# A graph-attention and feed-forward kernel: own rows added on TensorE, the merge of block ends beside the last store, both stages in one program block

## The chip, the core and the metric

The kernel runs on one core of a Trainium2 chip. The metric is the device time of one execution in microseconds. A core has five engines with a queue of instructions each: TensorE (PE in the profile), VectorE (DVE), ScalarE (ACT), GpSimd (POOL) and SyncE (SP), which here only issues transfers. They synchronise by semaphores.

## What is computed

`x` holds 6250 nodes of 256 features, and 206,250 directed edges, sorted by destination, join them. Stage one is a graph attention with four heads of 64, stage two 30 passes of a small feed-forward scan.

```python
x = x + relu(gat(layernorm(x)) + bias)
#   h = layernorm(x) @ W; e = leaky_relu(a_src[src] + a_dst[dst])
#   alpha = softmax of e over the edges of one dst; out[dst] = sum of alpha * h[src]
def step(h):                       # 30 times, starting from layernorm(x)
    h = h + 0.01 * tanh(h)
    h = h * sigmoid(h)
    h = layernorm(h) * w + b
    return h @ W.T + bias
x = x + scan(step)
```

## The kernel before

Stage one, `attention`. Each of the 128 partitions owns 1612 consecutive edges. In 124 steps of 13 edges POOL gathers the rows `haug[src]` into `G`, and DVE and ACT turn them into running softmax sums within a node. SP stores every step's rows to `sums` in DRAM (L398), so that `sums` at a node's last edge holds its maximum, its weights' sum and its weighted rows. At the end ACT copies the last running row of each partition into `tail` (L514), and SP waits until the last stores have landed (L401). Then the block of `attention` ends, with a barrier of all engines (L882), and the block of `scan_ffn` begins.

The merge. A node whose edges begin in one partition and end in a later one needs the parts of the earlier partitions. POOL gathers the row concerned of each partition from `sums` into `last_row` (L1033). DVE, PE and ACT broadcast the tails' maxima over the partitions (`tdiag`, L1332), mask and reduce them (`tm`, `tmax`), take exponentials (`tw`), transpose them (L1336) and form the weighted sums of the tails (L1340). DVE scales and adds, and POOL scatters `fixed` back to `sums` (L1036). All the gathers that follow wait for this scatter.

The batches. The 49 nodes of each partition go in seven batches of seven tiles (a tile is 128 nodes, one in each partition). For a batch, POOL gathers seven rows `S` from `sums` (`ends`, L1043). DVE forms the softmax shares (`shares`, `norms`) with one exponential by ACT between them, and ends them with `partw`. The node's own row (its self loop) is loaded by SP into `own`, in three buffers (L1019). ACT scales it in place with 28 instructions (`own_part`, L1105), DVE scales the gathered sums into `Hs` (L1229) and adds `own` to `Hs` (L1234). Then `added` takes the relu and adds `X` (L1241), and takes statistics (L1244, L1248, L1251). POOL computes the root with four instructions (`roots`, L1050 to L1056), and ACT normalises (L1113). In POOL's queue `roots(b)` stands behind the gathers of batch b + 3; in ACT's queue `normalise(b)` stands behind `own_part(b + 2)`.

The loops. 25 chunks of two tiles (the last has one) run 30 times: tanh on ACT (L1143), an add on POOL (L1072), silu on ACT (L1128), transposes on PE (L1348), a copy on ACT (L1133), the product on PE (L1356), statistics on DVE, the root on POOL (L1081) and the affine step on DVE (L1285).

The core of the two lines that the batches turn on:

```python
v.tensor_tensor(hs, hs, tile_heads(own[:, b % OW, :, :], HR), ALU.add).then_inc(s_agg, 1)        # L1234
ch.add(v.scalar_tensor_tensor(out=xs, in0=hs, scalar=0.0, in1=xs, op0=ALU.max, op1=ALU.add))     # L1241
```

## Time and profile before

| | |
|---|---|
| median of 3 runs | 4212.8 us (4206.08 to 4213.14) |
| the profiled execution | 4199.51 us, its span 4197.7 us |
| PE busy in the span | 1679.0 us (40%) |
| DVE busy | 3153.5 us (75%) |
| ACT busy | 2543.4 us (61%) |
| POOL busy | 3170.6 us (76%) |
| mean granted clock of TensorE | 0.704 |

Times in the rows below are microseconds from the start of the span. The profiled execution took 1.8 us more than its span and 13.3 us less than the median of the runs. A view by stretch shows three parts: stage one up to about 2443.7 us, the merge and the batches up to about 2574 us, and the 30 passes of the loops behind them. The granted clock is a share of TensorE's 2.4 GHz: 0.5 is 1.2 GHz.

### The profile page before, as it was taken

The numbers are of one execution on the slowest core, as the hardware profiler recorded it, in microseconds if no ns is written. First come the engines' busy times: TensorE is split into PE (matmuls) and PEld (weight loads), VectorE is DVE, ScalarE is ACT, GpSimd is POOL, SyncE is SP. The second block draws the span as 40 slices with busy tenths as digits, with TensorE's granted clock in tenths as the row PEclk, the third lists the DMA queues.
The fourth block names the chain that finished last, engine by engine and source line by source line (L and its number), as shares of the span: only waits on it lengthen the run. The fifth ranks groups of instructions, "written<-read, shape, count | busy, mean of one in ns | idle before, by whom it ended". The sixth has DMA issues, their size and how long they took to land. (4 is left out here: it accounts for less than half of the span.)

```text
span 4197.7 us, 52564 instructions
## 1 busy us (share of the span) xinstructions
PE 1679.0 (40%) x9142; PEld 1465.3 (35%) x9142; DVE 3153.5 (75%) x7419; ACT 2543.4 (61%) x4454; POOL 3170.6 (76%) x3312
## 2 busy tenths in 40 slices
PE   3400000000000000000000004999999999999997
PEld 2300000000000000000000003888888888888886
DVE  6476667667666677766767758888888888888887
ACT  4354455545455555545555548777777777777775
POOL 7676666766666667766666748999999999999996
PEclk8655555555555555555555556999999999999998
DMA  6365556656555556555666641000000000000001
GB/s 192 118 206 180 175 194 208 200 184 197 184 192 196 188 196 217 189 176 191 199 198 199 216 140 31 1 0 0 0 0 0 0 0 0 0 0 0 0 0 61
DMA packets 126628, 485.80 MB, mean 116 GB/s; under 512 B 50089, under 2 KB 52170, under 8 KB 110532
## 3 DMA queue, kind: packets, MB, share of 16 engines
q0 software_dynamic: 83824, 230.16, 18.9%
q1 hardware_dynamic: 41188, 253.75, 16.6%
q10 hardware_dynamic: 1536, 1.18, 0.1%
q14 instruction: 74, 0.61, 0.0%
q8 instruction: 6, 0.10, 0.0%
HBM read 249.79 MB, written 235.99 MB: 116 GB/s over the span
## 5 line engine op out<-in xcount | busy, mean ns | idle before, releaser
L581 POOL DMA_INDIRECT G<-haug,idx x1612 | 1524.6, 946 | 717.0 <-issue 581.2
L1356 PE MATMUL ps_g<-WT,S 128*128 128x256 f32 x5880 | 1394.9, 380 | 0.0
L477 ACT ACTIVATE G<-RS 128x845 f32<-128x845 f32 x496 | 852.1, 1718 | 651.5 <-issue 479.9
L1356 PEld LDWEIGHTS ps_g<-WT,S 128*128 128x128 f32 x5880 | 1060.0, 190 | 113.5
L813 DVE TENSOR_TENSOR_SCAN RS<-keep,psum 128x845 f32<-128x845 f32 x496 | 941.4, 1901 | 0.4
L1072 POOL TENSOR_TENSOR S<-Hs,S 128x512 f32<-128x512 f32 (+1 forms) x750 | 938.3, 1251 | 3.3 <-ACT S L1143 3.2
L1332 PE MATMUL ps_x<-tdiag,ones 128*128 128x512 f32 x2 | 2.1, 1140 | 2274.9 <-DVE tdiag L1176 2274.9
L1285 DVE SCALAR_TENSOR_TENSOR Hs<-ps_g,r,b 128x256 f32 (+1 forms) x1470 | 683.5, 465 | 181.9 <-PE ps_g L1356 170.7
L1332 PEld LDWEIGHTS ps_x<-tdiag,ones 128*128 128x128 f32 x2 | 0.5, 309 | 2275.1 <-DVE tdiag L1176 2275.1
L1081 POOL TENSOR_TENSOR r<-cve,half_neg 128x2 f32<-128x2 f32 (+1 forms) x750 | 525.5, 701 | 147.0 <-DVE cve L1277 123.1
L1133 ACT ACTIVATE S<-ps_x 128x512 f32<-128x512 f32 (+1 forms) x750 | 441.0, 588 | 313.5 <-PE ps_x L1348 308.4
L1264 DVE BATCH_NORM_STATS2 cst<-S 128x6 f32<-128x256 f32 x1470 | 547.6, 412 | 10.0 <-issue 4.4
L795 DVE TENSOR_TENSOR psum<-G,psum 128x845 f32<-128x845 f32 x496 | 478.2, 1032 | 17.3 <-ACT psum L461 7.7
L1348 PE MATMUL ps_x<-ident,S 128*128 128x128 f32 x2940 | 445.2, 273 | 113.7 <-ACT S L1128 113.6
L1128 ACT ACTIVATE S<-S 128x512 f32<-128x512 f32 (+1 forms) x750 | 461.8, 616 | 33.5 <-POOL S L1072 26.1
L1143 ACT ACTIVATE S<-Hs 128x512 f32 (+2 forms) x750 | 461.0, 615 | 4.3
L804 DVE SCALAR_TENSOR_TENSOR psum<-carried,KEEP,psum 128x260 f32<-128x260 f32 x123 | 60.7, 494 | 526.6 <-remote 452.3
L1348 PEld LDWEIGHTS ps_x<-ident,S 128*128 128x128 f32 x2940 | 368.6, 141 | 190.9 <-ACT S L1128 115.1
L472 ACT ACTIVATE carried<-RS,decay 128x65 f32<-128x65 f32 x492 | 157.9, 392 | 224.4 <-remote 209.4
L1277 DVE TENSOR_SCALAR cve<-cmv 128x2 f32<-128x2 f32 (+1 forms) x750 | 250.2, 334 | 1.1
L1271 DVE BATCH_NORM_AGGREGATE cmv<-cst 128x2 f32<-128x6 f32 x1470 | 175.8, 160 | 0.4
L461 ACT ACTIVATE psum<-el 128x56 f32<-128x56 f32 x124 | 27.8, 224 | 221.8 <-issue 151.4
(153 smaller groups left out, 1110.4 us busy)
## 6 DMA issues: line engine op xcount, KB each, us to landing
sums<-G SPq DMA_DIRECT2D x124, 1716.0 KB
G<-haug,idx POOLq DMA_INDIRECT x1612
haug<-G SPq DMA_DIRECT2D x7, 924.0 KB
own<-haug SPq DMA_DIRECT2D x7, 924.0 KB, 4.7
X<-x SPq DMA_DIRECT2D x7, 784.0 KB
out<-X SPq DMA_DIRECT2D x7, 784.0 KB
adz<-G SPq DMA_DIRECT2D x4, 830.5 KB
G<-adz SPq DMA_DIRECT2D x1, 3224.0 KB, 11.5
```

The lines of the kernel that those rows point to most:

```text
L477: nc.scalar.activation(G[:, k % R, :, h * HR:(h + 1) * HR].rearrange("p t f -> p f t"), RS[:, h, :, :], ACT.Copy).then_inc(s_rows, 1)
L581: pool.indirect_dma_start(out=G[:, u, t, :], out_offset=None, in_=haug[:, :], in_offset=bass.IndirectOffsetOnAxis(ap=idx[:, u, t:t + 1], a ...
L795: ch.add(v.tensor_tensor(ps_m[:, h, :, :].rearrange("p f t -> p t f"), G[:, u, :, h * HR:(h + 1) * HR], w, ALU.mult))
L813: v.tensor_tensor_scan(RS[:, h, :, :].rearrange("p f t -> p (f t)"), keep[:, k % 2, :, :].rearrange("p f t -> p (f t)"), ps_m[:, h, :, :]. ...
L1072: g.tensor_tensor(h1[:, u, 0:w * C], chunk_rows(Hs, j0 + u, w), th[:, u, 0:w * C], ALU.add).then_inc(s_add, 1)
L1081: g.tensor_tensor(r100[:, u, 0:w], cve[:, u, 0:w], half_neg[:, 0:w], ALU.pow).then_inc(s_r, 1)
L1128: nc.scalar.activation(h2[:, u, 0:w * C], h1[:, u, 0:w * C], ACT.Silu, scale=1.0 / HS).then_inc(s_silu, 1)
L1143: nc.scalar.activation(th[:, u, 0:w * C], chunk_rows(Hs, j0 + u, w), ACT.Tanh, scale=1.0 / HS).then_inc(s_tanh, 1)
L1264: last = v.bn_stats(cst[:, u, a, :], h2[:, u, a * C:(a + 1) * C])
L1285: ins = v.scalar_tensor_tensor(out=Hs[:, bass.ds(j * CH + a, 1), :].rearrange("p a c -> p (a c)"), in0=ps_g[u][:, a * C:(a + 1) * C], scal ...
L1348: last = nc.tensor.transpose(ps_x[XB[u]][:, n * P:(n + 1) * P], h2[:, u, n * P:(n + 1) * P], ident[:, :])
L1356: last = nc.tensor.matmul(ps_g[u][:, a * C:(a + 1) * C], h2T[:, u, (a * 2 + k) * P:(a * 2 + k + 1) * P], WT[:, k, :], start=(k == 0), stop ...
```

## The change

Four edits. (1) The two blocks become one: `attention` and `scan_ffn` return their five queue programs, and one block runs one behind the other on each engine, without a barrier between. (2) The merge becomes the end of `attention`. Its scratch tiles lie in a part of `AD`. It takes the exponentials against the earlier partitions' own maximum `tmax`, so that they don't need `last_row`, and rescales both parts with `escale` afterwards. POOL itself waits for the stores. SP, POOL and DVE wait for `s_merged` at the start of stage two, so that the loads of `own`, which had been issued at the start of the second block, now come behind the merge. (3) DVE no longer adds `own` to `Hs`: TensorE multiplies the identity with the rows of `Hs` and of `own` into the same PSUM region (14 products a batch), and the relu reads this sum. The order of DVE's work becomes `gathered(b)` and then `added(b - 1)`. (4) The scale of the root moves into DVE's `ve`, and the sign of the mean into a new `nmean`, so that `roots` has two instructions in place of four. PSUM is laid out anew for the loops, and the first transposes and the first product wait until the batches' sums are read.

```diff
-        attention(nc, sem, res, dram, x, src, dst, gW, att_src, att_dst, gbias, ln_w, ln_b, fW, fb)
-        scan_ffn(nc, sem, res, dram, out)
+        *attend, s_merged = attention(nc, sem, res, dram, x, src, dst, gW, att_src, att_dst, gbias, ln_w, ln_b, fW, fb)
+        iterate = scan_ffn(nc, sem, res, dram, out, s_merged)
+        with nc.Block() as block:
+            @block.sync
+            def _(sp):
...
+                attend[0](sp)
+                iterate[0](sp)
...
-            for u in range(R):
-                sp.wait_ge(s_st[u], TURNS * 16)
...
+        def gpsimd_fix(pool):
+            for u in range(R):
+                pool.wait_ge(s_st[u], TURNS * 16)
+            pool.indirect_dma_start(out=last_row, out_offset=None, in_=sums[:, :],
+                                    in_offset=bass.IndirectOffsetOnAxis(ap=e1_idx[:, 0:1], axis=0)).then_inc(s_e1, 16)
+            pool.wait_ge(s_fixed, 1)
+            pool.indirect_dma_start(out=sums[:, :], out_offset=bass.IndirectOffsetOnAxis(ap=e1_idx[:, 0:1], axis=0),
+                                    in_=fixed, in_offset=None).then_inc(s_merged, 16)
...
+        def scalar_fix(act):
+            act.wait_ge(s_tlog, 1)
+            nc.scalar.activation(tw, tm, ACT.Exp).then_inc(s_tw, 1)
+            act.wait_ge(s_twT, 1)
+            nc.scalar.activation(twT.rearrange("p h q -> p (h q)"), ps_twT, ACT.Copy).then_inc(s_twc, 1)
+            act.wait_ge(s_ediff, 1)
+            nc.scalar.activation(escale, ediff, ACT.Exp).then_inc(s_escale, 1)
...
+            dve.wait_ge(s_tail, 1)
+            for h in range(H):
+                last = v.tensor_scalar(tdiag[:, h, :], ident[:, :], tail[:, SUMS + h:SUMS + h + 1], None, ALU.mult)
+            last.then_inc(s_tdiag, 1)
+            dve.wait_ge(s_trow, 1)
+            ch.add(v.tensor_tensor(tm, ps_trow.rearrange("p (h q) -> p h q", h=H),
+                                   maskneg[:, :].unsqueeze(1).to_broadcast([P, H, P]), ALU.add))
+            ch.wait()
+            v.tensor_reduce(tmax, tm, axis=AX.X, op=ALU.max).then_inc(s_tmax, 1)
+            dve.wait_ge(s_tmax, 1)
+            v.tensor_tensor(tm, tm, tmax.unsqueeze(2).to_broadcast([P, H, P]), ALU.subtract).then_inc(s_tlog, 1)
+            dve.wait_ge(s_e1, 16)
+            ch.add(v.tensor_tensor(emax, tmax, last_row[:, SUMS:ROW], ALU.max))
+            ch.wait()
+            v.tensor_tensor(ediff[:, 0, :], last_row[:, SUMS:ROW], emax, ALU.subtract)
+            v.tensor_tensor(ediff[:, 1, :], tmax, emax, ALU.subtract).then_inc(s_ediff, 1)
+            v.tensor_copy(fixed[:, SUMS:ROW], emax)
+            dve.wait_ge(s_escale, 1)
+            v.tensor_tensor(heads(fixed), heads(last_row), escale[:, 0, :].unsqueeze(2).to_broadcast([P, H, HR]), ALU.mult)
+            dve.wait_ge(s_tsum, 1)
+            ch.add(v.tensor_tensor(heads(earlier), heads(ps_tsum), escale[:, 1, :].unsqueeze(2).to_broadcast([P, H, HR]), ALU.mult))
+            ch.wait()
+            v.tensor_tensor(fixed[:, 0:SUMS], fixed[:, 0:SUMS], earlier[:, 0:SUMS], ALU.add).then_inc(s_fixed, 1)
...
+        psum = ctx.enter_context(nc.psum_tensor("ps", [P, 8 * 512], F32))
+        assert QT * C <= 4 * 512 and NQ % 2 and U == 5
+        ps_sum = [psum[:, n * 2048:n * 2048 + QT * C] for n in range(2)]
+        ps_g = [psum[:, n * 512:(n + 1) * 512] for n in (0, 1, 2, 3, 7)]
+        ps_x = [psum[:, n * 512:(n + 1) * 512] for n in (4, 5, 6)]
...
+            sp.wait_ge(s_merged, 16)
...
+            pool.wait_ge(s_merged, 16)
...
+            def roots(b):
+                t0, t1 = part_tiles(b)
+                pool.wait_ge(s_x1var, b + 1)
+                ch.add(g.tensor_tensor(rstd[:, t0:t1], ve[:, t0:t1], half_neg[:, t0:t1], ALU.pow))
...
+                g.tensor_tensor(nmr[:, t0:t1], rstd[:, t0:t1], nmean[:, t0:t1], ALU.mult).then_inc(s_x1root, 1)
...
+            dve.wait_ge(s_merged, 16)
...
+            def gathered(b):
+                hs = tile_heads(Hs[:, b * QT:(b + 1) * QT, :], HID)
+                dve.wait_ge(s_part, b + 1)
+                v.tensor_tensor(hs, tile_heads(S[:, b * QT:(b + 1) * QT, :], HR),
+                                part[:, b % 2, 0, :, :].unsqueeze(3).to_broadcast([P, QT, H, HID]),
+                                ALU.mult).then_inc(s_scaled, 1)
...
+            def added(b):
+                t0, t1 = part_tiles(b)
+                xs = X[:, t0:t1, :].rearrange("p t c -> p (t c)")
+                dve.wait_ge(s_agg, b + 1)
+                v.scalar_tensor_tensor(out=xs, in0=ps_sum[b % 2], scalar=0.0, in1=xs, op0=ALU.max, op1=ALU.add).then_inc(s_added, 1)
+                dve.wait_ge(s_added, b + 1)
...
+                v.tensor_scalar(nmean[:, t0:t1], mv[:, t0:t1, 0], -1.0, None, ALU.mult)
+                v.tensor_scalar(ve[:, t0:t1], mv[:, t0:t1, 1], EPS, 1.0 / (HS * HS), ALU.add, ALU.mult).then_inc(s_x1var, 1)
...
+            for b in range(NQ):
+                shares(b)
+                norms(b)
+                gathered(b)
+                if b:
+                    added(b - 1)
+            added(NQ - 1)
...
+            def add_own(b):
+                pe.wait_ge(s_scaled, b + 1)
+                pe.wait_ge(s_ownw, b + 1)
+                wait_count(pe, s_added, b - 1)
+                for j in range(QT):
+                    to = heads(ps_sum[b % 2][:, j * C:(j + 1) * C], HID)
+                    nc.tensor.matmul(to, ident[:, :], heads(Hs[:, b * QT + j, :], HID), start=True, stop=False)
+                    last = nc.tensor.matmul(to, ident[:, :], heads(own[:, b % OW, j, :], HR), start=False, stop=True)
+                last.then_inc(s_agg, 1)
+
+            for b in range(NQ):
+                add_own(b)
...
+            def transposes(q, u, w):
+                if isinstance(q, int) and q == 0:
+                    pe.wait_ge(s_added, NQ - 1)
...
+            def product(q, u, w):
+                if isinstance(q, int) and q == 0:
+                    pe.wait_ge(s_added, NQ)
```

Rows of a queue are written as line, operation, output<-inputs and size. In the changed kernel the merge's scratch is named `AD`, and PSUM `psum` or `ps`; its line numbers are its own.

DVE, from the second batch on (batch 1 in the code), before: `partw` closes `norms(1)`, and then come `added(0)`, `gathered(1)` and the start of `shares(2)`.

```order
L1219 TENSOR_TENSOR partw<-share,den 128x56
L1241 SCALAR_TENSOR_TENSOR X<-Hs,X 128x1792
L1244 BN_STATS bst<-X 128x6 x7
L1248 BN_AGGR mv<-bst 128x2 x7
L1251 TENSOR_SCALAR ve<-mv 128x7
L1229 TENSOR_TENSOR Hs<-S,partw 128x1792
L1234 TENSOR_TENSOR Hs<-Hs,own 128x1792
L1205 TENSOR_TENSOR nmax<-S,eself 128x28
```

The same place on DVE in the changed kernel:

```order
L1273 TENSOR_TENSOR partw<-share,den 128x56
L1282 TENSOR_TENSOR Hs<-S,partw 128x1792
L1290 SCALAR_TENSOR_TENSOR X<-ps,X 128x1792
L1293 BN_STATS bst<-X 128x6 x7
L1297 BN_AGGR mv<-bst 128x2 x7
L1300 TENSOR_SCALAR nmean<-mv 128x7
L1301 TENSOR_SCALAR ve<-mv 128x7
L1259 TENSOR_TENSOR nmax<-S,eself 128x28
```

The addition of `own` is gone from DVE, the scaling of `S` stands ahead of the relu of the batch before, and the relu reads PSUM.

POOL, from the end of stage one to the second group of roots, before:

```order
L882 UNCONDITIONAL_BRANCH
L1029 UNCONDITIONAL_BRANCH
L1033 DMA last_row<-sums,e_idx 128x264
L1036 DMA sums<-fixed,e_idx 206337x264
L1043 DMA S<-sums,end_idx 128x264 x28
L1050 TENSOR_TENSOR rstd<-ve,half_neg 128x7
L1052 ISA
L1052 TENSOR_SCALAR rstd<-rstd 128x7
L1054 TENSOR_TENSOR nmr<-rstd,mv 128x7
L1056 TENSOR_SCALAR nmr<-nmr 128x7
L1043 DMA S<-sums,end_idx 128x264 x7
L1050 TENSOR_TENSOR rstd<-ve,half_neg 128x7
```

The same place on POOL in the changed kernel:

```order
L935 DMA AD<-sums,e_idx 128x264
L938 DMA sums<-AD,e_idx 206337x264
L1130 DMA S<-sums,end_idx 128x264 x28
L1137 TENSOR_TENSOR rstd<-ve,half_neg 128x7
L1139 TENSOR_TENSOR nmr<-rstd,nmean 128x7
L1130 DMA S<-sums,end_idx 128x264 x7
L1137 TENSOR_TENSOR rstd<-ve,half_neg 128x7
```

The branches out of and into a block are gone, and each group of roots has two instructions; the order of gathers and roots is the same.

PE, between stage one and the loops, before:

```order
L879 MATMUL psum<-bdiag,ones 128x128 x2
L882 UNCONDITIONAL_BRANCH
L1329 UNCONDITIONAL_BRANCH
L1332 MATMUL ps_x<-tdiag,ones 128x512
L1336 MATMUL ps_x<-ident,tw 128x128 x4
L1340 MATMUL ps_x<-tail,twT 128x65 x4
L1348 MATMUL ps_x<-ident,S 128x128 x12
```

The same place on PE in the changed kernel, up to the second tile of the first batch:

```order
L925 MATMUL psum<-bdiag,ones 128x128 x2
L951 MATMUL psum<-AD,ones 128x512
L954 MATMUL psum<-ident,AD 128x128 x4
L958 MATMUL psum<-tail,AD 128x65 x4
L1389 MATMUL ps<-Hs,ident 128x256
L1390 MATMUL ps<-own,ident 128x256
L1389 MATMUL ps<-Hs,ident 128x256
L1390 MATMUL ps<-own,ident 128x256
```

The pair of L1389 and L1390 comes 49 times in all, ahead of the first transposes of the loops.

## Rows read from the trace of the kernel before

**Rows 1.** Busy time by stretch: PE, PEld, DVE, ACT, POOL; then PEclk, DMA share, GB/s

```profile
2455.00:2458.00 3.00, 0.00 (x0) 0.00 (x0) 1.00 (x4) 0.25 (x2) 0.00 (x0) 0.50 1.03 430
...
2596.00:4171.00 1575.00, 1575.00 (x8724) 1388.16 (x8725) 1385.18 (x5100) 1222.19 (x2222) 1426.39 (x1483) 1.00 0.00 0
```

**Rows 2.** Timeline of the merge: start, duration, engine, line, operation, idle time before

```profile
2443.30 0.42 ACT L514 ACTIVATE tail<-G 128x264 f32<-128x264 f32 x1
...
2449.37 0.87 DVE L1176 TENSOR_SCALAR tdiag<-ident,tail 128x128 f32<-128x128 f32 x4 [7.85 <-PEq L882]
...
2453.13 0.69 DVE L1183 TENSOR_REDUCE tmax<-tm 128x4 f32<-128x512 f32 x1
...
2457.03 0.68 DVE L1190 TENSOR_TENSOR tm<-tm,emax 128x512 f32<-128x512 f32 x1
...
2458.50 0.43 DVE L1193 TENSOR_TENSOR fixed<-last_row,escale 128x260 f32<-128x260 f32 x1 [0.79 <-ACT tw L1091]
...
2460.33 1.97 PE L1340 MATMUL ps_x<-tail,twT 128*128 128x65 f32 x8 [0.69 <-ACT twT L1093]
...
2465.83 0.96 POOL L1043 DMA_INDIRECT S<-sums,end_idx  x1 [1.72 <-DMA sums<-fixed,e_idx]
```

**Rows 3.** Chain of work: start, duration of the merge's two transfers

```profile
2449.97 6.62 DMA last_row<-sums,e_idx
...
2463.11 2.46 DMA sums<-fixed,e_idx
```

**Rows 4.** Waits of SP's queue around the merge: total, times, longest

```profile
SPq L401 <- DMA sums<-G: 5.1, 1, 5.1
```

**Rows 5.** Timeline of one batch in the middle, all engines

```profile
2526.82 3.55 ACT L1113 ACTIVATE Hs<-X,nmr,rstd 128x256 f32<-128x256 f32 x7 [3.04 <-POOL nmr L1056]
...
2531.49 2.02 DVE L1241 SCALAR_TENSOR_TENSOR X<-Hs,X 128x1792 f32<-128x1792 f32 x1
2531.67 6.79 ACT L1105 ACTIVATE own<-own,partw 128x64 f32<-128x64 f32 x28 [1.17 <-issue]
2532.11 2.22 POOL L1043 DMA_INDIRECT S<-sums,end_idx  x1 [0.30 <-issue]
2533.54 2.39 DVE L1244 BATCH_NORM_STATS2 bst<-X 128x6 f32<-128x256 f32 x7
...
2536.66 2.02 DVE L1229 TENSOR_TENSOR Hs<-S,partw 128x1792 f32<-128x1792 f32 x1
2536.85 3.21 POOL L1050 TENSOR_TENSOR rstd<-ve,half_neg 128x7 f32<-128x7 f32 x1
2538.71 2.02 DVE L1234 TENSOR_TENSOR Hs<-Hs,own 128x1792 f32<-128x1792 f32 x1
...
2541.51 3.55 ACT L1113 ACTIVATE Hs<-X,nmr,rstd 128x256 f32<-128x256 f32 x7 [3.04 <-POOL nmr L1056]
```

**Rows 6.** Timeline of the last batch, POOL, ACT and DVE

```profile
2556.12 1.51 POOL L1050 TENSOR_TENSOR rstd<-ve,half_neg 128x7 f32<-128x7 f32 x1
...
2561.04 6.79 ACT L1105 ACTIVATE own<-own,partw 128x64 f32<-128x64 f32 x28 [1.17 <-DVE partw L1219]
...
2570.13 2.02 DVE L1241 SCALAR_TENSOR_TENSOR X<-Hs,X 128x1792 f32<-128x1792 f32 x1
```

**Rows 7.** Timeline of a step of stage one, DVE and POOL

```profile
2224.91 3.85 DVE L795 TENSOR_TENSOR psum<-G,psum 128x845 f32<-128x845 f32 x4
2225.47 0.94 POOL L581 DMA_INDIRECT G<-haug,idx  x1 [0.30 <-issue]
```

**Rows 8.** Timeline of PE at the start of the loops

```profile
2577.10 1.11 PE L1348 MATMUL ps_x<-ident,S 128*128 128x128 f32 x4 [0.26 <-ACT S L1128]
2578.01 3.62 PE L1356 MATMUL ps_g<-WT,S 128*128 128x256 f32 x8
...
2588.50 1.89 PE L1356 MATMUL ps_g<-WT,S 128*128 128x256 f32 x8
```

**Rows 9.** Stretches of 1 us, PE alone: busy, granted clock, DMA share, GB/s

```profile
2581.00:2582.00 1.00, 1.00 (x7) 0.67 0.00 0
```

683 lines of the change are left out of this document (315 added, 368 removed).

## The prediction

> **What bounds the kernel now.** I read the busy time by stretch first. In the loops PE is busy for 1575.0 of 1575 us at the full clock, while DVE, ACT and POOL have room [rows 1]. The change leaves the loops' instructions as they are, so nothing is to be had there, and the question is when the loops start. The timeline shows what lies ahead of them. Stage one ends with the copy of `tail` at 2443.72, the first gather of stage two starts at 2465.83 [rows 2], and the first product of the loops at 2578.01 [rows 8]. I count batch times from that first gather, as +x: the product is at +112.2.
>
> In the middle of the batches one batch takes 2541.51 - 2526.82 = 14.69 us [rows 5]. POOL has no idle time in it: seven gathers of 1.25 us (0.95 and 0.30 between) make 8.75; one that runs into a DVE instruction is stretched to 2.22, 1.27 more; and the roots take 2541.51 - 2536.85 = 4.66, of which 3.21 is the power. Sum 14.68. So POOL sets the pace. ACT needs only 3.55 + 1.30 (from the end of the normalisation to the start of `own_part`, for shares and norms) + 6.79 = 11.64 us [rows 5].
>
> **The merge.** Now it is a chain in series: the store lands 5.1 us after SP began to wait for it [rows 4], which I put at 2448.8; then come the barrier, the gather of `last_row` (6.62 us) and, behind it, subtraction, exponential, transposes and products, and the scatter (2.46 us) [rows 2, 3].
> In the new order two chains run side by side from 2443.72.
> - Tails: `tdiag` to `tmax` took 2453.82 - 2449.37 = 4.45, and the subtraction to the last product 2462.30 - 2457.03 = 5.27 [rows 2]. With 0.05 for starts this chain is done at 2453.5.
> - `last_row`: the store at 2448.8, then the gather. Its 6.62 us were spent beside three loads of `own` that filled the DMA engines (share 1.03 [rows 1]); the scatter of the same rows without them took 2.46 [rows 3]. The loads now come later, so I take 3.0 and keep 2.46 and 6.62 as bounds: 2451.8. Four small DVE instructions, an exponential and a scaling of 0.43 [rows 2] are put at 1.3 us: 2453.1.
>
> The tails end last, at 2453.5. Two DVE instructions of 0.43, 0.27 to start, 2.46 for the scatter and 0.26 to the first gather give 2457.4. Against 2465.83 this is **8.4 us**. With 6.62 for the gather it would be 5.3 us.
> The loads of `own` now start with the gathers and not 16 us ahead. I cost this at nothing: the first `own` is wanted only at +12.4 (below), and the first loads shared the DMA with `last_row` and that landed in 6.62. If the first batch came 2 us late for it, the next batches would absorb it, since ACT idles between `own_part(0)` and the shares of batch 1, which wait for gathers.
>
> **The batches.**
> - DVE loses one addition of 2.02 a batch. What counts is who waited on DVE's account. The power of 1.51 us [rows 6] takes 3.21 when it meets L1229 and L1234, and a gather takes 2.22 when it meets L1241 [rows 5]: each time DVE reads two SBUF operands. L1234 is gone, and L1241 now has one operand in PSUM. In stage one DVE's L795, with one operand in PSUM, runs for 3.85 us over a gather that takes 0.94 [rows 7]. So I let only L1229 stretch a gather, by 1.3 a batch, and the power stays at 1.51, since DVE runs no such instruction right behind `ve` any more. The Trainium skill, "SBUF — State Buffer", section "Who interferes with whom", says that a VectorE instruction with at most one SBUF input leaves GpSimd alone, and the trace agrees. The same section infers that a `tensor_tensor` does not hold up the descriptors of a GpSimd transfer. By that the gathers would never be stretched, and the POOL cycle below would be 1.3 us shorter; the 2.22 us speak against it.
> - Roots: 4.66 becomes 1.51 + 0.08 + 0.21 and a start, 1.85 us. `nmean` adds 0.1 on DVE, beside POOL's gathers.
> - POOL's cycle: 8.75 + 1.3 + 1.85 = 11.9. ACT's: 11.64. I take 12.0.
> - PE: a batch has 14 products of 256 columns. Four of them (eight instructions) show 1.89 us at the full clock and 3.62 at half [rows 8], with an end that overlaps the next; in a row of 14 I take 0.44 and 0.88 each. At the start of the loops the clock rose at about 2581.6, 4.6 us after work without gaps began at 2577.10 [rows 8, 9]. If it does so in each addition, 4.6 us give 5.2 products and the other 8.8 take 3.9: **x = 8.5 us**. Bounds: 6.2 all at full, 12.3 all at half.
> - Is the addition on the path? It starts when `own_part(b)` ends. Then come x us for it, 2.05 for the relu, 3.4 for statistics and variance, 0.5 for the shares of batch b + 2, 1.3 to the start of their `own_part` and 6.8 for that: x + 14.1 for two batches. With x = 8.5 that is 11.3 a batch, under 12.0. It becomes the bound from x = 9.9.
>
> Times: 28 gathers with three stretched take 38.9; with `roots(0)`, normalisation(0) starts at +41, ends at +44.6, and `own_part(3)` starts at +45.9. Three cycles later `own_part(6)` starts at **+81.9**; before, it was 2561.04, +95.2 [rows 6].
>
> **The start of the loops.** `own_part(6)` ends at +88.7, the addition at +97.2, the relu at +99.3, and the first product may start at +99.4, 12.8 us earlier than +112.2. But DVE is not as far: before, its last relu ended at 2572.15, +106.3 [rows 6], now at +99.3, 7.0 us earlier, and statistics, variances and affine steps hang on it. POOL's addition for chunk 4 stands behind the root of chunk 0, which needs DVE. So the first products come earlier by 12.8, and then PE waits. By the fifth product I expect 9.1 us, between the bounds 7.0 and 12.8. From there PE is never idle in either kernel but for a wait of about 1 us.
>
> **Sum:** 8.4 + 9.1 = 17.5 us. The profiled execution's 4199.5 would become 4182.0, its span 4180.2. The median of the runs lies 13.3 higher: 4212.8 - 17.5 = **4195.3 us**, 0.42% less.
>
> **Rivals.** 0.2% is 8.4 us, about what a measurement of this kernel can tell from no change.
> - *The additions stay at half clock* (chance 0.12). Between two batches PE idles for some 3.5 us, and after long idle time it started the loops at half clock. x = 12.3: `own_part(6)` then ends at 19.2 + 3 * (x + 14.1) = +98.4, where 19.2 is the end of `own_part(0)` (seven gathers 8.75, landing 1.9, shares 1.8, and 6.8). That is 9.7 later than +88.7, and the last addition 3.8 longer: 17.5 - 13.5 = 4.0 us faster, 4208.8. Against it stands that the clock did rise within 4.6 us of steady work. The Trainium skill, "TensorE: Matmul & The Clock Gate", section "HAM oscillation — how this bites in real kernels", tells of kernels that fall back to the low clock in each gap and start each burst slowly; that is the forecast for each batch's first part, and this rival if the rise never comes.
> - *The additions stream more slowly than the loops' products* (0.07), and the kernel ends slower. Their operands and results are cut into four pieces of 64, `own` at a stride of 65, which no row shows. At twice the time, x = 14.6: +105.3, so 16.6 and 6.1 lost, 5.2 us slower than before, 4218.0. It decides from x = 13.3, and is slower by 0.2% from x = 15.4 (1.1 us a product). For it: nothing but the absence of a row. Against: L795 and L1229 show no price for such cuts, on another engine though.
> - *The merge gains little* (0.08): the gather of `last_row` is slow by itself. 5.3 + 9.1 = 14.4 us, 4198.4, inside the range.
> - *The loops run a little slower* (0.05): PSUM banks and the place of the code have moved. PE has 750 chunks (1575 us for 8724 / 12 = 727 of them, 2.17 each) with no slack at all [rows 1], so 23 ns a chunk eat the 17.5 us, and 35 ns make it slower by 0.2%. No row speaks for it.
> - The forecast: 0.68. Its own range is 4188 to 4203.
>
> **Numbers.** The range takes in the bounds of the merge (5.3 to 9), of the batches (POOL unstretched gives 2 us more) and of the loops' start (7.0 to 12.8), a few us between sets of runs, and reaches to the first rival: 4184 to 4209. Faster by over 0.2%: the forecast, the third rival and a part of the first, 0.80; within 0.2%: 0.14; slower: 0.06.
>
> **What would show it.** In the profile after: `tdiag` right behind `tail`, and the first gather of `S` 13.7 us behind `tail`; gathers over 2 us only beside the scaling of `S`, and powers of 1.5 us; 12 us from one normalisation to the next; additions of 8 to 9 us with the clock rising in each; a gap of PE after the second or third product. It is wrong if the additions take over 10 us, if DVE's relu from PSUM still holds up POOL, if the last store lands later than 2449, or if a chunk of the loops no longer takes what it did.

## The result, and the profile after

The changed kernel takes 4190.9 us, the median of 5 runs (4188.57 to 4197.38); the kernel before, run beside it, takes 4211.19 us (5 runs, 4206.08 to 4213.14). The ratio is 0.996, with a 95% interval of 0.9949 to 0.9972: faster by 0.3 to 0.5%. The forecast was 4195.3 us. One run of the kernel before, on the chip of e5_warm to e9_old_order below, took 6804.12 us where its other 19 took 3956 to 3961; it is a slow one and no ratio uses it.

Its profiled execution took 4197.38 us, its span 4195.2 us at a mean granted clock of 0.711. PE is busy for 1731.7 us, DVE for 3150.6, ACT for 2550.9, POOL for 3159.0.

The span is only 2.5 us shorter than before, and the reason lies ahead of the change. In this execution stage one ended 14.8 us later: the copy of `tail` ended at 2458.50, before at 2443.72 [rows 2]. Other kernels below, with the same stage one and on chips on which it ran as long, ended it anywhere from 2439.6 to 2457.6. So I compare executions from the end of `tail` on: 1753.98 us before, 4195.2 - 2458.50 = 1736.70 after, **17.28 us less; the sum of the prediction was 17.5**. Times "+x" count from the first gather of `S`, as in the prediction.

**The merge.** The timeline of the changed kernel:

```profile
2458.07 0.43 ACT L560 ACTIVATE tail<-G 128x264 f32<-128x264 f32 x1
...
2458.53 0.87 DVE L968 TENSOR_SCALAR AD<-ident,tail 128x128 f32<-128x128 f32 x4 [2.24 <-ACT tail L560]
...
2464.36 0.94 POOL L935 DMA_INDIRECT AD<-sums,e_idx  x1 [42.57 <-DMA sums<-G]
...
2466.23 1.97 PE L958 MATMUL psum<-tail,AD 128*128 128x65 f32 x8 [0.69 <-ACT AD L945]
...
2468.71 0.43 DVE L988 TENSOR_TENSOR AD<-AD 128x260 f32<-128x260 f32 x1
...
2472.14 0.97 POOL L1130 DMA_INDIRECT S<-sums,end_idx  x1 [1.73 <-DMA sums<-AD,e_idx]
```

The tails' work starts 0.03 us behind `tail`, while the last store is still on its way; before, it waited for the new block [rows 2]. The first gather comes 13.64 us behind `tail`, where it was 22.11. The chain of waits (start, duration, what) shows which of the two chains ends last:

```profile
2458.11 5.48 DMA sums<-G
...
2463.66 0.70 issue
2464.36 2.74 DMA AD<-sums,e_idx
...
2468.71 0.44 DVE AD L988
2469.15 0.27 issue
2469.41 2.47 DMA sums<-AD,e_idx
```

By this view it goes through the store and `last_row`. The products of the tails end at 2468.20, 0.06 us before the scaling of `last_row` does (2467.83 + 0.43 = 2468.26): the two chains end level, and which of them is last is too close to call, as the ends of products are modelled in the profile. The gather of `last_row` took 2.74 us, before 6.62 [rows 3]; the scatter 2.47, as before.

**The batches.** One batch in the middle:

```profile
2515.13 3.56 ACT L1189 ACTIVATE Hs<-X,nmr,rstd 128x256 f32<-128x256 f32 x7
...
2515.34 1.19 PE L1389 MATMUL ps<-Hs,ident 128*128 128x256 f32 x2 [7.21 <-issue]
...
2519.94 2.03 DVE L1282 TENSOR_TENSOR Hs<-S,partw 128x1792 f32<-128x1792 f32 x1
2520.00 6.82 ACT L1181 ACTIVATE own<-own,partw 128x64 f32<-128x64 f32 x28 [1.17 <-issue]
...
2520.82 1.97 POOL L1130 DMA_INDIRECT S<-sums,end_idx  x1 [0.31 <-issue]
...
2522.82 1.52 POOL L1137 TENSOR_TENSOR rstd<-ve,half_neg 128x7 f32<-128x7 f32 x1
...
2523.79 0.59 PE L1390 MATMUL ps<-own,ident 128*128 128x256 f32 x2
...
2524.42 2.02 DVE L1290 SCALAR_TENSOR_TENSOR X<-ps,X 128x1792 f32<-128x1792 f32 x1 [2.45 <-PE ps L1390]
2524.78 1.01 POOL L1130 DMA_INDIRECT S<-sums,end_idx  x1 [0.16 <-issue]
...
2526.71 3.57 ACT L1189 ACTIVATE Hs<-X,nmr,rstd 128x256 f32<-128x256 f32 x7
```

A batch takes 2526.71 - 2515.13 = 11.58 us, before 14.69 [rows 5]. The power takes 1.52 instead of 3.21. The gather that runs into the scaling of `S` (L1282, two operands in SBUF) is stretched to 1.97; the one that starts 0.36 us into the relu, which now reads PSUM (L1290), takes 1.01. This addition lasted from 2515.34 to 2524.38, 9.04 us; the others of this execution took 6.3 to 9.3. The granted clock, the sixth number behind the stretch and its length (PE, PEld, DVE, ACT and POOL busy stand between), shows why. The first three lines are of this addition, the next two of the one after it:

```profile
2517.00:2518.00 1.00, 1.00 (x3) 0.76 (x3) 0.90 (x9) 1.00 (x3) 0.94 (x1) 0.50 0.47 131
2520.00:2521.00 1.00, 1.00 (x4) 0.77 (x4) 1.00 (x1) 1.00 (x5) 0.69 (x2) 0.53 0.36 114
2521.00:2522.00 1.00, 1.00 (x6) 0.90 (x5) 0.97 (x1) 1.00 (x6) 1.00 (x1) 1.00 0.53 135
...
2525.00:2527.00 2.00, 0.08 (x1) 0.11 (x2) 1.97 (x3) 2.00 (x9) 1.70 (x2) 1.00 0.83 225
2528.00:2531.00 3.00, 3.00 (x9) 2.34 (x8) 2.52 (x17) 2.53 (x6) 2.21 (x3) 0.50 0.60 200
...
2600.00:4170.00 1570.00, 1570.00 (x8696) 1383.75 (x8694) 1391.82 (x5082) 1222.30 (x2212) 1423.32 (x1477) 1.00 0.00 0
```

The addition began at half clock (0.50 is 1.2 GHz) and had the full clock from about 2520.9, 5.6 us after its start. PE had idled for 7.2 us before it. The next one, at 2526.92 and behind 2.54 us of idle time, began at the full clock, fell to half some 0.8 us into its work and had the full clock again from about 2531.2, so that it took 7.96 us. The last line is the loops: PE has no idle time in them, as before [rows 1]. From the tenth product to the end of the span it is 1596.4 us, before 1596.9.

**The start of the loops.** PE in the changed kernel, and POOL's root of chunk 0:

```profile
2572.18 1.99 PE L1412 MATMUL ps<-WT,S 128*128 128x256 f32 x8 [0.23 <-DVE X L1290]
...
2574.45 1.89 PE L1412 MATMUL ps<-WT,S 128*128 128x256 f32 x8
...
2576.72 0.70 POOL L1164 TENSOR_TENSOR r<-cve,half_neg 128x2 f32<-128x2 f32 x1 [4.91 <-DVE cve L1327]
...
2579.38 1.12 PE L1402 MATMUL ps<-ident,S 128*128 128x128 f32 x4 [3.03 <-ACT S L1204]
2580.28 2.93 PE L1412 MATMUL ps<-WT,S 128*128 128x256 f32 x8
...
2586.36 1.89 PE L1412 MATMUL ps<-WT,S 128*128 128x256 f32 x8
```

The first product is at +100.0, 12.1 us earlier than before. Behind the second PE idles for 3.03 us, because POOL waited 4.91 us for DVE's variances of chunk 0, and the third product runs at half clock (2.93 us). The fifth is at +114.2, 8.5 us earlier.

### The profile page after: what moved, and what is told of

It reads as the page before. It is cut to its first block, busy times and chain, and to the rows that moved or that the text cites. A ratio compares the mean times of both kernels' runs of the same rounds, so it can differ in the third digit from the quotient of the medians.

```text
span 4195.2 us, 52930 instructions
## 1 busy us (share of the span) xinstructions
PE 1731.7 (41%) x9338; PEld 1508.3 (36%) x9338; DVE 3150.6 (75%) x7421; ACT 2550.9 (61%) x4454; POOL 3159.0 (75%) x3298
## 4 chain that ended last, share of the span: by engine, by line
PE 40%; DVE 16%; another core or an unknown queue 15%; issue 12%; POOL 8%; DMA 4%; SPq 2%; ACT 1%; DVEq 0%; ACTq 0%; POOLq 0%
PE ps L1412 30%; DVE RS L859 9%; PE ps L1402 8%; POOL G L627 8%; DVE psum L841 5%; DMA sums<-G 2%; SPq L399 1%; DMA G<-haug,idx 1%; PE psum L909 1%; PE ps L1389 1%; SPq L437 1%; PE ps L1390 1%; ACT G L523 0%; DVE bm L825 0%
## 5 line engine op out<-in xcount | busy, mean ns | idle before, releaser
L1412 PE MATMUL ps<-WT,S 128*128 128x256 f32 x5880 | 1394.2, 380 | 0.2 <-DVE X L1290 0.2
L1412 PEld LDWEIGHTS ps<-WT,S 128*128 128x128 f32 x5880 | 1059.7, 190 | 113.8 <-DVE X L1290 0.5
L1335 DVE SCALAR_TENSOR_TENSOR Hs<-ps,r,b 128x256 f32 (+1 forms) x1470 | 684.3, 466 | 172.0 <-PE ps L1412 161.5
L1164 POOL TENSOR_TENSOR r<-cve,half_neg 128x2 f32<-128x2 f32 (+1 forms) x750 | 526.4, 702 | 148.7 <-DVE cve L1327 124.4
L1209 ACT ACTIVATE S<-ps 128x512 f32<-128x512 f32 (+1 forms) x750 | 442.4, 590 | 307.6 <-PE ps L1402 301.1
L1402 PE MATMUL ps<-ident,S 128*128 128x128 f32 x2940 | 444.0, 273 | 5.2 <-ACT S L1204 4.7
L1402 PEld LDWEIGHTS ps<-ident,S 128*128 128x128 f32 x2940 | 368.5, 141 | 81.8 <-ACT S L1204 6.6
L1327 DVE TENSOR_SCALAR cve<-cmv 128x2 f32<-128x2 f32 (+1 forms) x750 | 262.9, 350 | 1.1
```

The lines of the kernel that those rows point to most:

```text
L1164: g.tensor_tensor(r100[:, u, 0:w], cve[:, u, 0:w], half_neg[:, 0:w], ALU.pow).then_inc(s_r, 1)
L1335: ins = v.scalar_tensor_tensor(out=Hs[:, bass.ds(j * CH + a, 1), :].rearrange("p a c -> p (a c)"), in0=ps_g[u][:, a * C:(a + 1) * C], scal ...
L1402: last = nc.tensor.transpose(ps_x[XB[u]][:, n * P:(n + 1) * P], h2[:, u, n * P:(n + 1) * P], ident[:, :])
L1412: last = nc.tensor.matmul(ps_g[u][:, a * C:(a + 1) * C], h2T[:, u, (a * 2 + k) * P:(a * 2 + k + 1) * P], WT[:, k, :], start=(k == 0), stop ...
```

## The experiments

They ran on three chips, on one of which stage one took some 250 us less; what is compared below stands on one chip, or is a distance within an execution. The columns: median of the runs, its ratio to the kernel before on the same chip with the 95% interval, then of the profiled execution the first gather behind `tail`, the end of the span behind `tail`, and the fifth and the tenth product of the loops behind the first gather. The kernel before had a median of 4208.41 us on the chip of e1 to e4, 3958.83 on that of e5, e6, e7 and e9, and 4211.63 on that of c1, e8 and e10.

| kernel | us | ratio | 1st gather | end | 5th | 10th |
|---|---|---|---|---|---|---|
| before | 4211.19 | 1 | 22.11 | 1753.98 | +122.7 | +135.0 |
| after | 4190.9 | 0.9960 [0.9949, 0.9972] | 13.64 | 1736.70 | +114.2 | +126.6 |
| e1_merge_only | 4201.44 | 0.9978 [0.9964, 0.9991] | 13.63 | 1744.39 | +123.1 | +135.3 |
| e2_undo_pe | 4196.51 | 0.9966 [0.9953, 0.9979] | 13.67 | 1742.81 | +120.6 | +132.9 |
| e3_undo_roots | 4195.23 | 0.9966 [0.9955, 0.9977] | 13.64 | 1738.97 | +116.7 | +129.2 |
| e4_loads_late | 4209.45 | 1.0002 [0.9992, 1.0011] | 19.26 | 1750.85 | +123.2 | +135.5 |
| e5_warm | 3940.88 | 0.9955 [0.9938, 0.9971] | 13.63 | 1735.52 | +112.0 | +124.4 |
| e6_reorder | 3944.01 | 0.9965 [0.9951, 0.9979] | 13.65 | 1739.52 | +110.8 | +129.4 |
| e7_double | 3959.69 | 1.0004 [0.9994, 1.0014] | 13.64 | 1754.49 | +132.0 | +144.4 |
| e9_old_order | 3968.54 | 1.0025 [1.0015, 1.0034] | 13.62 | 1762.75 | +140.3 | +152.7 |
| c1_after | 4195.1 | 0.9962 [0.9948, 0.9975] | 13.64 | 1738.28 | +117.1 | +127.9 |
| e8_warm_reorder | 4192.99 | 0.9959 [0.9946, 0.9973] | 13.64 | 1734.29 | +110.4 | +124.6 |
| e10_spread | 4189.26 | 0.9943 [0.9929, 0.9957] | 13.64 | 1731.47 | +110.8 | +121.6 |

Two executions of the same changed kernel (after and c1_after) differ by 1.6 us in the distance from `tail` to the end, so differences under about 2 us in that column say little by themselves.

**c1_after: the changed kernel once more**, without an edit, beside the last two.

> The changed kernel again. Theory: the stretch from the tail copy to the end of the span is 1736 to 1737.5 us as in its first profile (1736.70), and the end of stage one may lie anywhere within some 15 us, as it did for kernels with the same stage one. Rival (the change delays stage one, as the first profiles suggested): the tail copy ends about 15 us later than in the kernels with the old stage two.

It took 4195.1 us beside 4211.63, 16.5 us less. The additions took 6.3 to 9.2 us again, a batch 11.55. The distance from `tail` to the end, 1738.28 us, is 0.8 over the 1736 to 1737.5 that I expected, and its fifth product comes 2.9 us later than in after. 1.1 of them were there at the first product, since the last addition took 9.22 us for 7.76; behind it two products ran almost wholly at half clock (3.21 and 3.22 us) where after had one. The rival, that the change delays stage one, finds no support: `tail` ended at 2454.62 here, at 2454.05 in e4_loads_late with the old stage two, and at 2439.59 in e2_undo_pe, which has the new merge.

**e1_merge_only: the one block and the merge alone.** The additions are back on DVE, the old order and the old roots too.

```diff
             for b in range(NQ):
                 shares(b)
                 norms(b)
-                gathered(b)
                 if b:
                     added(b - 1)
+                gathered(b)
...
-            for b in range(NQ):
-                add_own(b)
```

> The changed kernel with DVE adding own and with four root instructions, so that only the merge and the single block are left of the change. My theory (two terms, 8.4 for the merge and 8.5 for the batches and the start of the loops): from the end of the tail copy to the first gather of S 13.6 us as in the changed kernel (22.1 before), from there to the fifth product 122.7 us as before (114.2 in the changed kernel); time 8 to 9 us under the kernel before. Rival (the single block also helps or hurts stage one or the loops): the two intervals are as said and the time is off by more than 5 us.

The first gather stands at 13.63 us, as in the whole change, and the batches are those of before: 14.70 us each, fifth product at +123.1. From `tail` to the end it is 9.6 us less than before, 8.5 of them ahead of the first gather. The rest of the gain, 7.7 us against after and 6.1 against c1_after, belongs to the other edits. The loads of `own` come behind the merge here too, and so the runs show what that costs: `own_part(0)` starts at +13.5, before at +12.3, and `own_part(6)` at +95.6, before at +95.2. With the additions on DVE 0.4 of the 1.2 us are left.

**e2_undo_pe: the additions back on DVE and the old order, with the new roots**

> The changed kernel with DVE adding own to Hs again, in the old order; merge and two-instruction roots stay. Theory (DVE's instructions with two SBUF operands hold POOL up, and POOL sets the pace): the power takes 2.6 to 3.2 us again, gathers over 2 us appear beside the relu, one batch takes 13.6 to 14 us against 11.7, and the fifth product comes 119 to 122 us after the first gather against 114.2. Rival (the roots' shorter chain was what gained): batches of about 12.5 us, fifth product at 116.

The edit is that of e1_merge_only, but for the roots, which stay at two instructions. A batch took 14.13 us, a little more than the 13.6 to 14 that I expected; the fifth product, at +120.6, is where I expected it. POOL and DVE in the middle of one:

```profile
2518.70 2.34 POOL L1130 DMA_INDIRECT S<-sums,end_idx  x1 [0.30 <-issue]
...
2523.43 2.02 DVE L1282 TENSOR_TENSOR Hs<-S,partw 128x1792 f32<-128x1792 f32 x1
2523.56 3.27 POOL L1137 TENSOR_TENSOR rstd<-ve,half_neg 128x7 f32<-128x7 f32 x1
2525.49 2.03 DVE L1287 TENSOR_TENSOR Hs<-Hs,own 128x1792 f32<-128x1792 f32 x1
```

The power meets the two DVE instructions with two SBUF operands each, and takes 3.27 us. So two POOL instructions fewer gave only 14.70 - 14.13 = 0.57 us a batch; the power of 1.5 us comes with the new place of the addition and the new order together. e9_old_order below parts the two.

**e3_undo_roots: the old four instructions of the root, the rest as changed**

```diff
-                g.tensor_tensor(nmr[:, t0:t1], rstd[:, t0:t1], nmean[:, t0:t1], ALU.mult).then_inc(s_x1root, 1)
+                ch.add(g.tensor_scalar(rstd[:, t0:t1], rstd[:, t0:t1], HS, None, ALU.mult))
+                ch.wait()
+                ch.add(g.tensor_tensor(nmr[:, t0:t1], rstd[:, t0:t1], mv[:, t0:t1, 0], ALU.mult))
+                ch.wait()
+                g.tensor_scalar(nmr[:, t0:t1], nmr[:, t0:t1], -1.0, None, ALU.mult).then_inc(s_x1root, 1)
...
```

On DVE `nmean` and the scale in `ve` go too.

> The changed kernel with four root instructions again. Theory: roots take 0.65 us longer on POOL, whose cycle of 11.7 is level with ACT's, so a batch takes 12.3 to 12.5 us and the fifth product comes 2 to 3 us later (116 to 117.5 us after the first gather). Rival (ACT alone sets the pace and POOL has room): batches stay at 11.7, fifth product within 1 us of 114.2.

A batch took 11.55 us at first and 12.7 later, 1.1 more than after; the power stays at 1.53. From `tail` to the end it is 2.3 us more than after, 0.7 more than c1_after. The start of `own_part(6)` shows it more clearly, since it lies ahead of the clock's ups and downs at the start of the loops: +84.6 here, +83.2 in after, +82.9 in c1_after, so that the new roots are worth 1.4 to 1.7 us there. The batch of 11.55 and then 12.7 us also tells the two limits apart. From one power to the next POOL takes 12.8 us, without idle time. As long as POOL was ahead, ACT set the pace; once the lead was used up, POOL did.

**e4_loads_late: the kernel before, with the loads of `own` behind the merge**

```diff
             def _(sp):
+                sp.wait_ge(s_merged, 16)
                 for b in range(NQ):
```

> The kernel before with one wait more: SP issues the loads of own behind the merge. Theory (the gather of last_row was slow only because it shared the DMA with them): it lands in 2.7 us in place of 6.6, the first gather of S comes 3.9 us earlier after the tail copy (18.2 us), and the time is 3 to 4 us less, so that nearly half of the merge's 8.4 us is had with one line. Rival (the wait hurts the first batch): first gather as said, but the fifth product later than 123.7 us after it, and no gain in time.

The timeline of its merge, POOL and DVE:

```profile
2460.28 0.95 POOL L1034 DMA_INDIRECT last_row<-sums,e_idx  x1 [43.47 <-POOLq L882]
...
2463.44 0.69 DVE L1184 TENSOR_REDUCE tmax<-tm 128x4 f32<-128x512 f32 x1
2464.16 0.16 DVE L1187 TENSOR_TENSOR emax<-tmax,last_row 128x4 f32<-128x4 f32 x1
```

The view of the tile gives 2.8 us from the issue to the landing of `last_row`, where it was 6.62 [rows 3]: the loads beside it were what made it slow. But the first gather comes only 22.11 - 19.26 = 2.85 us earlier: with the row there at about 2463.1, `emax` waits for `tmax`. The wait was hidden behind one that was nearly as long. From `tail` to the end it is 3.1 us less than before, 0.07%, which the interval of the ratio allows; the runs alone can't tell this kernel from before. The other 5.6 us of the merge's 8.5 come from the single block and from the tails' work beside the store, which no run took apart.

**e5_warm: TensorE kept busy between two additions**, with products of no use into free PSUM

```diff
+            def fill(b, count):
+                pe.wait_ge(s_added, b)
+                spare = psum[:, (1 - b % 2) * 2048 + QT * C:(2 - b % 2) * 2048]
+                for _ in range(count):
+                    nc.tensor.matmul(spare, ident[:, :], WT[:, 0, :], start=True, stop=True)
+
             for b in range(NQ):
                 add_own(b)
+                if b < NQ - 1:
+                    fill(b, (1, 14, 9, 10, 10, 11)[b])
```

> The changed kernel with products of no use (identity with weights, into columns of PSUM that nothing reads) in the gaps between the additions, 1, 14, 9, 10, 10 and 11 of them. Theory (additions are slow only at half clock, and only the last is on the path): every addition from the second takes 6.1 us, the first product of the loops comes 1.7 us earlier (98.3 us after the first gather against 100.0), a batch stays at 11.7, the fifth product comes 1 to 2 us earlier. Rival (additions are on the path in each batch): batches get shorter too and the fifth product comes 4 us or more earlier.

PE, and a stretch over the same time:

```profile
2260.29 0.67 PE L1389 MATMUL ps<-Hs,ident 128*128 128x256 f32 x2 [1.26 <-issue]
...
2266.41 4.05 PE L1397 MATMUL ps<-WT,ident 128*128 128x256 f32 x18
2271.83 0.67 PE L1389 MATMUL ps<-Hs,ident 128*128 128x256 f32 x2 [1.37 <-issue]
```

```profile
2260.00:2272.00 12.00, 10.33 (x47) 8.86 (x48) 9.00 (x33) 10.83 (x38) 9.90 (x10) 1.00 0.56 168
```

With gaps of 1.3 us the clock stays at 1.00, and each addition from the second on takes 6.28 us, the prediction's bound with all products at full clock. So the clock is the whole of what x lies above 6.2, and the cuts into pieces of 64 cost nothing. A batch took 11.55 us all the same, 0.03 less than the one shown of after. In the middle batches the addition is on the path only where it is longest: in after the starts of `own_part` behind the additions of 9.04 and 9.32 us are 11.75 and 12.04 us apart, the others from `own_part(2)` on 11.6, and so `own_part(6)` starts at +82.6 here and at +83.2 there. The last addition is on the path whole, 6.28 us for 7.76. Together it ends 2.2 us earlier. The first product, which here waits for ACT, gains 1.0 us of that (+99.0; I had expected +98.3), the fifth all 2.2.

**e7_double: each addition made twice** (the same sums, 28 products)

```diff
-                for j in range(QT):
+                for j in (*range(QT), *range(QT)):
```

> The changed kernel with every addition done twice over (28 products a batch, the second time starting anew), so that an addition takes about 14 us in place of 8. It gives the same sums. Theory (an addition becomes the bound from about 10 us, then each us costs half a us a batch and one at the end): batches of about 14.1 us, the first product of the loops about 22 us later than in the changed kernel (20 to 24), and the kernel slower than before by 3 to 6 us. Rival (additions are hidden and only the last counts): 6 to 7 us later.

Stretches between the first pair of additions and the second, in the second, and at the start of the last:

```profile
2264.00:2266.00 2.00, 0.03 (x1) 0.06 (x1) 1.97 (x2) 2.00 (x9) 1.40 (x2) 1.00 0.77 177
2266.00:2278.00 12.00, 12.00 (x56) 10.50 (x56) 6.59 (x24) 10.36 (x37) 10.04 (x9) 1.00 0.43 150
...
2320.00:2322.00 2.00, 2.00 (x7) 1.56 (x6) 1.97 (x12) 2.00 (x6) 0.00 (x0) 0.50 0.00 0
```

Additions follow each other in pairs here. Behind 2.17 and 2.13 us of idle time the clock stays at full, and 28 products take 12.2 us; behind 2.10 us it falls some 0.3 us into the last addition, which takes 14.0. The batches took 12.13 and 14.44 in turn, 13.3 on average. The prediction's (x + 14.1) / 2 gives (12.2 + 14.1) / 2 = 13.15. Its point at which the addition becomes the bound, x = 9.9, came from a pace of 12.0; with the 11.55 measured the same sum gives 9.0, which fits the two additions of after named above. What I expected of this kernel was off, since I had put its additions at about 14 us: the first product comes 17.8 us later than in after, not 20 to 24, and it is not 3 to 6 us slower than before. The whole kernel comes out level with before (1.0004): with additions of 12 to 14 us the change no longer pays.

**e9_old_order: the changed kernel with DVE's order of before**

```diff
             for b in range(NQ):
                 shares(b)
                 norms(b)
-                gathered(b)
                 if b:
                     added(b - 1)
+                gathered(b)
```

> The changed kernel with DVE's old order in a batch, added(b - 1) ahead of gathered(b). Theory (neither is on the path, since ACT and POOL set the pace): batches of 11.7 us, fifth product within 1 us of 114.2. Rival (the new order is part of the gain): the scaling of S stands behind the relu, which waits for PE, so the additions start late, and the fifth product comes 3 us or more later.

The timeline of this kernel from one scaling of `S` to the next:

```profile
2266.32 2.02 DVE L1282 TENSOR_TENSOR Hs<-S,partw 128x1792 f32<-128x1792 f32 x1
2266.49 3.23 POOL L1137 TENSOR_TENSOR rstd<-ve,half_neg 128x7 f32<-128x7 f32 x1 [1.67 <-DVE ve L1301]
2268.39 1.22 PE L1389 MATMUL ps<-Hs,ident 128*128 128x256 f32 x2 [7.35 <-DVE Hs L1282]
...
2279.73 2.38 DVE L1293 BATCH_NORM_STATS2 bst<-X 128x6 f32<-128x256 f32 x7
...
2282.91 2.02 DVE L1282 TENSOR_TENSOR Hs<-S,partw 128x1792 f32<-128x1792 f32 x1
```

This is slower than before (1.0025, interval above 1), and its fifth product comes 26 us later than in after, 23 later than in c1_after. I had held that the order is not on the path; that was wrong, and the rival right. The rows show a ring: the scaling of batch b ends at 2268.34, the addition starts 0.05 us later and takes 9.2 us, and the relu, the statistics and `ve` follow; the scaling of batch b + 1 stands behind them on DVE, 2282.91 - 2266.32 = 16.59 us later (15.1 to 16.6 in the middle batches), longer than the 14.69 of before. PE waits 7.35 us for DVE, and the power meets the scaling again (3.23 us), though DVE's addition is gone: that the power takes 1.52 us in the changed kernel is due to the order, which moves the scaling away from behind `ve`. **The order of DVE's work, which looked like a detail, carries the gain of the batches:** the addition on TensorE pays only because `gathered(b)` no longer waits for the sum of batch b - 1. What the new order would give with the additions left on DVE was not run.

**e6_reorder: the last batch's statistics and root moved behind those of the first chunks**

```diff
-                if isinstance(q0, int) and q0 == 0:
-                    roots(NQ - 1)
+                    if isinstance(q, int) and q == 8:
+                        roots(NQ - 1)
...
-                    added(b - 1)
-            added(NQ - 1)
+                    summed(b - 1)
+                    measured(b - 1)
+            summed(NQ - 1)
...
                 variance(q, q, CH)
+            measured(NQ - 1)
```

> The changed kernel with DVE taking the variances of the first three chunks ahead of the statistics of the last batch, and POOL taking the last roots behind chunk 8 in place of chunk 4. Theory (the gap of PE behind the second product comes from POOL's add for chunk 4 behind the root of chunk 0 behind DVE's statistics): the 3.0 us gap and the half-clock product behind it vanish, the fifth product comes 4 to 5 us earlier (109 to 110 us after the first gather against 114.2), and the ninth 3 to 5 us earlier. Rival (ACT's copies or the late statistics hold PE up anyway): the gap moves behind the fifth product and the ninth product gains under 1 us.

The timeline of PE and ACT around its seventh and eighth product:

```profile
2326.95 1.89 PE L1417 MATMUL ps<-WT,S 128*128 128x256 f32 x8
...
2328.12 3.55 ACT L1189 ACTIVATE Hs<-X,nmr,rstd 128x256 f32<-128x256 f32 x7 [1.44 <-POOL nmr L1139]
...
2332.76 1.11 PE L1407 MATMUL ps<-ident,S 128*128 128x128 f32 x4 [3.92 <-ACT S L1204]
```

The gap behind the second product shrinks, and the fifth product comes at +110.8. But the last normalisation then waits 1.44 us for its root and holds ACT for 3.55, PE idles for 3.92, and the product behind the gap runs at half clock (3.62 us). The tenth product is at +129.4, 2.8 later than in after, 1.5 later than in c1_after. The gap had only moved, as the rival had it.

**e8_warm_reorder: the fill and the new order together**, the root behind chunk 6 and not 8.

> The changed kernel with the products of no use between the additions, the first three variances on DVE ahead of the last batch's statistics, and the last roots on POOL behind chunk 6 (behind chunk 8 the last normalisation on ACT waited for them). Theory: the last roots end early enough for ACT, the fifth product comes 108 to 110 us after the first gather against 114.2, the tenth at 121 to 123 against 126.6, and the stretch from tail copy to end takes 1732 to 1734 us. Rival (the gap moves again to the last normalisation): tenth product within 1.5 us of the changed kernel's.

Its edits are those of e5_warm and e6_reorder. The fifth product is at +110.4, 0.4 us later than the latest that I expected, the tenth at +124.6, 1.6 us later than the latest expected for it, since the last normalisation still stands as one block of 3.54 us in ACT's queue ahead of chunk 7, and PE waits 2.22 us there. From `tail` to the end it is 4.0 us less than c1_after.

**e10_spread: the same, with the normalisations of the last two batches spread over the chunks**, one or two tiles behind each

```diff
-            def normalise(b):
+            def normalise(b, some=None):
...
+            def spread(b, first, cuts):
+                return lambda u: normalise(b, cuts[u - first]) if u >= first else None
...
+            first_turn(0, 0, FIRST, spread(NQ - 2, 1, ((0, 2), (2, 4), (4, 5), (5, 7))))
+            first_turn(U, U, MID, spread(NQ - 1, 3, ((0, 1), (1, 2))))
+            first_turn(2 * U, 2 * U, MID, spread(NQ - 1, 0, ((2, 3), (3, 4), (4, 5), (5, 6), (6, 7))))
```

> As the kernel with both edits, and ACT spreads the 14 normalisations of the last two batches over the chunks of the first three turns, one or two a chunk, in place of two blocks of 3.6 us. Theory (PE's remaining wait behind the seventh product is ACT busy with the last block): that wait of 1.3 us goes and the tenth product comes 1 to 2 us earlier still, 1731 to 1733 us from tail copy to end. Rival (ACT is as late with the pieces, since its queue is in order and nearly full): no gain over the other.

The timeline of PE at the start of its loops:

```profile
2572.19 3.06 PE L1429 MATMUL ps<-WT,S 128*128 128x256 f32 x8
...
2575.53 1.89 PE L1429 MATMUL ps<-WT,S 128*128 128x256 f32 x8
...
2577.69 1.89 PE L1429 MATMUL ps<-WT,S 128*128 128x256 f32 x8
```

The first product runs mostly at half clock (3.06 us), and from the second on they follow without a gap, one every 2.16 us; the tenth comes at +121.6. From `tail` to the end it is 1731.47 us, 6.8 less than c1_after beside it and 5.2 less than after. Its median, 4189.26, is the lowest of the three on this chip; the intervals of the ratios overlap, so that it beats the changed kernel is shown by the trace, not by the runs. Against e8_warm_reorder, which has all but the spreading, it is 2.8 us less, and the tenth product comes 3.0 earlier: that is the spreading. The other 4.0 us are the fill and the new order together, which were not taken apart on this chip.

## Why the prediction was right, point by point

- **The merge** was put at 8.4 us and gave 8.47 (13.64 us from `tail` to the first gather, predicted 13.7); e1_merge_only gave it alone. The store landed 5.09 us behind `tail` (2463.59), where 5.1 was put, so the late absolute time is only that of stage one. Of the two chains that of the tails ended at 9.70, put at 9.8. That of `last_row` was put at 9.4 and ended at 9.76: POOL's gather started 0.70 us behind the end of its wait, for which I had put nothing, and against that the gather took 2.74 instead of 3.0 and the small instructions behind it 1.16 instead of 1.3. That this 0.4 us cost nothing is luck, as the tails were as late. The bound of 6.62 us, and the rival that the gather is slow by itself, fell with e4_loads_late.
- **The loads of `own` at nothing** was not quite right. `own` itself landed in 4.6 us, but a gather of the first batch beside the three loads took 6.20 us, `own_part(0)` started at +13.5 and not +12.4, and in this kernel it was not absorbed as I had said: the first addition starts when `own_part(0)` ends, at +20.4 for 19.2. With the additions on DVE it is absorbed but for 0.4 us (e1_merge_only).
- **The batches.** 12.0 us were predicted, 11.58 measured. Every part of the cycle was as put, but the stretch of the gather, 1.0 for 1.3. What I missed is who sets the pace. I had POOL at 11.9 with ACT at 11.64 behind it; in the trace ACT goes without idle time from normalisation to `own_part`, with the shares' 1.3 us between, and POOL at 11.6 stays 2 us ahead. `normalise(0)` was put at +41, where POOL has the root; it started at +43.0, since ACT was still in `own_part(2)`, which hangs on the first addition. The prediction's own terms had this path: 19.2 for the end of `own_part(0)`, then x and the 14.1 behind it give 19.2 + 8.5 + 14.1 = +41.8, later than POOL's +41; the other 1.2 us are the loads. That and the faster cycle gave +83.2 for `own_part(6)`, where +81.9 was put. POOL's own cycle is as long as ACT's here, and e3_undo_roots shows that it sets the pace as soon as it is longer.
- **x = 8.5 us** was right in size (6.3 to 9.3, five of seven between 7.7 and 9.1) and that the clock is what lies above 6.2 is shown: e5_warm has 6.28 us where the clock stays. The course of the clock was right only in part. Behind idle time of 3.8 to 7.2 us the additions began at half clock; the two behind 2.5 and 2.3 us began at full and fell 0.8 and 1.4 us into their work. The full clock came 3.0 to 6.1 us after the start of an addition, where 4.6 were put for each, so that the mean of 8.1 us so near to 8.5 is partly luck. The first rival (half clock throughout) and the second (pieces of 64 stream more slowly) are refuted. The Trainium skill, "TensorE: Matmul & The Clock Gate", section "HAM oscillation — how this bites in real kernels", speaks of falling back to the low clock in the gap before each burst; the trace agrees where PE idles for 3.8 to 7.2 us. With gaps of 1.3 us e5_warm shows no fall; with 2.1 to 2.5 us there is none in two gaps of e7_double, and one soon after the work began in its third and in after.
- **What stretches POOL** was right: only DVE instructions with two SBUF operands did. The inference in the Trainium skill, "SBUF — State Buffer", section "Who interferes with whom", that a `tensor_tensor` doesn't hold up GpSimd's descriptors, is again not what the trace shows (1.97 us beside L1282, 0.95 alone); which part of the gather's work is held up, no run shows.
- **The start of the loops.** Predicted 12.8 us earlier for the first product, 9.1 for the fifth; measured 12.1 and 8.5, with 8.3 at the tenth (11.0, 5.6 and 7.1 in c1_after). The gap of PE came behind the second product with the cause put down for it, POOL waiting for DVE. That the third product would then run at half clock (about 1 us) I had not put down. There is luck in the first product: `own_part(6)` started 1.3 us late and the last addition took 7.76 us for 8.5. In c1_after it took 9.22, and the fifth product gained 5.6 us, below the 7.0 that I had as the lower bound for it.
- **The loops** run as they did, 1570.00 us busy of 1570; the fourth rival is refuted.
- **The sum:** 17.5 predicted, 17.28 and 15.7 in the two profiled executions from `tail` on, 20.3 and 16.5 by the medians of the two sets. In the first, 8.5 us are the merge's, 8.3 lie between the first gather and the tenth product, and 0.5 in the loops behind it. The medians hold stage one as well, whose end moves by more than the difference between them.
- **What the prediction did not speak of**, though the change described it: the new order on DVE. One term rests on it unsaid: the power at 1.51 us, "since DVE runs no such instruction right behind `ve` any more", holds by the order and not by the addition's leaving DVE (3.2 us in e9_old_order). The rest of it is in no term, as I took each engine's work per batch and the chain through `own_part`, in which the order stood as given. e9_old_order puts its worth, with the additions on TensorE, at 23 to 26 us, more than the whole gain.

## What to carry to other kernels

When work moves from one engine to another, first look at the order in which the old engine issues what feeds it: the addition taken off DVE lost more than it gave while the next operand was still queued behind its result (e9_old_order). Compare executions from a mark just ahead of the change, since what runs ahead of it may vary by more than the change is worth, as stage one did here. A gap can hide another of nearly the same length, as it did in e4_loads_late and e6_reorder: spread the blocking work in small pieces between the items, rather than move it as one block.

## What the runs showed of the hardware that was not expected

- Stage one, with the same instructions, ended 19 us apart in different executions (2439.6 to 2458.5), and some 250 us earlier on one chip of the three (2197.4 to 2203.8).
- A gather of rows lands in 2.7 to 2.8 us alone, and in 6.2 to 6.6 beside three loads of 924 KB each.
- With 28 products in place of 14 the mean time of one fell, from 9.04 / 14 = 0.65 us in the addition shown to 12.2 / 28 = 0.44, with the clock at 1.00 throughout. PE had idled for 7.2 us before the one and for 2.2 before the other.
- The same length of idle time left the clock at full or not: behind 2.17 and 2.13 us in e7_double it stayed, behind 2.10 it fell 0.3 us into the work, behind 2.54 and 2.27 in after 0.8 and 1.4 us into it.
